# Norms of two query heads in one run, and their scale moved from the scores to the exponential

## The reference, cut to what matters

```
def rmsnorm(x, g, eps=EPS):
    var = jnp.mean(jnp.square(x), axis=-1, keepdims=True)
    return x * jax.lax.rsqrt(var + eps) * g
scale = 1.0 / np.sqrt(D)
q = (hidden_states @ Wq).reshape(B, Sq, H, D)
k = (encoder_hidden_states @ Wk).reshape(B, Skv, H, D)
v = (encoder_hidden_states @ Wv).reshape(B, Skv, H, D)
q = rmsnorm(q, gq)
k = rmsnorm(k, gk)
scores = jnp.einsum('bqhd,bkhd->bhqk', q, k) * scale
attn = jax.nn.softmax(scores, axis=-1)
out = jnp.einsum('bhqk,bkhd->bqhd', attn, v)
return out.reshape(B, Sq, H * D) @ Wo
```

## Time and profile before

| | us |
|---|---|
| median of 3 runs | 1866.22 (1866.08 to 1866.52) |
| the profiled execution | 1869.1 |
| its span | 1867.3 |
| PE busy | 1758.7 (94%) |
| DVE busy | 1317.8 (71%) |
| ACT busy | 955.9 (51%) |
| POOL busy | 663.5 (36%) |

### The profile page before, as it was taken

The page is one execution under the profiler, slowest core; times in us unless marked ns, Lnnn a source line. Parts: engine busy times, 40 slices in busy tenths (PEclk is TensorE's granted clock), DMA queues, the critical chain, the costliest instruction groups (busy, mean ns, idle before and its releaser), DMA issues.

```text
span 1867.3 us, 19387 instructions
## 1 busy us (share of the span) xinstructions
PE 1758.7 (94%) x6054; PEld 801.7 (43%) x6054; DVE 1317.8 (71%) x1919; ACT 955.9 (51%) x1904; POOL 663.5 (36%) x693
## 2 busy tenths in 40 slices
PE   8878769989999999999999999999999899999999
PEld 2323233434444344444444544444444344454543
DVE  3978877998998799889887989987643444422221
ACT  6867875656563555575456565564435233330100
POOL 1324522345472244456432464562123333310100
PEclk9989889999999899999999999999999999999999
DMA  8999933688771146697312589841112799846110
GB/s 267 260 289 291 300 109 98 173 211 215 189 195 46 48 102 155 160 266 196 102 31 70 129 199 234 212 109 62 41 47 78 215 301 256 246 141 241 68 51 28
DMA packets 163173, 300.30 MB, mean 161 GB/s; under 512 B 18936, under 2 KB 51704, under 8 KB 160128
## 3 DMA queue, kind: packets, MB, share of 16 engines
q1 hardware_dynamic: 145792, 236.14, 40.3%
q0 software_dynamic: 17280, 62.92, 17.5%
HBM read 177.64 MB, written 58.33 MB: 126 GB/s over the span
## 4 chain that ended last, share of the span: by engine, by line
PE 62%; DVE 18%; issue 6%; ACT 5%; DMA 5%; POOL 2%; SPq 2%; DVEq 0%; ACTq 0%; POOLq 0%
PE p L799 9%; PE p L776 8%; PE p L759 8%; PE p L810 8%; PE p L846 6%; DVE s_M L963 5%; PE p L652 4%; PE p L782 4%; PE p L861 3%; DVE s_M L958 2%; PE p L699 2%; DVE s_M L968 2%; PE p L733 2%; DMA s_bc<-bc_scratch 1%; PE p L738 1%
## 5 line engine op out<-in xcount | busy, mean ns | idle before, releaser
L963 DVE TENSOR_TENSOR_SCAN s_M<-s_M 128x1024 f32<-128x1024 f32 x128 | 296.8, 2319 | 7.8 <-ACT s_M L1218 5.3
L1106 DVE CUSTOM_DVE_ANT_0 s_U<-p,s_U 128x512 f32<-128x512 f32 x256 | 187.3, 745 | 162.8 <-PE p L776 161.5
L776 PE MATMUL p<-s_U 128*128 128x512 f32 x512 | 269.3, 614 | 5.6 <-DVE s_U L1106 2.8
L759 PE MATMUL p<-s_U 128*128 128x512 f32 x512 | 253.7, 604 | 4.7 <-DMA s_U<-in_Wq 2.1
L1445 POOL DMA_DIRECT2D s_u<-s_M x120 | 112.6, 938 | 391.5 <-DVE s_M L968 368.8
L1490 POOL TENSOR_SCALAR s_U<-s_U 128x512 f32<-128x512 f32 x256 | 229.4, 917 | 6.3
L810 PE MATMUL p<-s_U 128*128 128x512 f32 x512 | 224.0, 593 | 0.0
L799 PE MATMUL p<-s_U 128*128 128x512 f32 x472 | 213.6, 593 | 2.6 <-ACT s_U L1348 2.5
L1348 ACT COPY s_U<-p 128x512 f32<-128x512 f32 x196 | 105.3, 592 | 189.7 <-PE p L782 188.4
L1218 ACT ACTIVATE s_M<-s_dl,s_small 128x511 f32<-128x511 f32 x256 | 170.3, 718 | 40.3 <-DVE s_M L963 36.8
L1343 ACT ACTIVATE s_U<-s_U 128x512 f32<-128x512 f32 x256 | 181.6, 710 | 5.3
(11 more groups left out here) (171 smaller groups left out, 2364.3 us busy)
## 6 DMA issues: line engine op xcount, KB each, us to landing
s_u<-s_M POOLq DMA_DIRECT2D x120, 512.0 KB, 7.6
s_bc<-bc_scratch SPq DMA_DIRECT2D x128, 256.0 KB, 5.0
k_scratch<-s_U SPq DMA_DIRECT2D x16, 1024.0 KB, 9.4
v_scratch<-s_U SPq DMA_DIRECT2D x16, 1024.0 KB, 7.8
s_U<-in_Wq SPq DMA_DIRECT2D x64, 256.0 KB, 6.9
s_U<-k_scratch SPq DMA_DIRECT2D x64, 256.0 KB, 5.2
s_U<-rk_scratch SPq DMA_DIRECT2D x64, 256.0 KB, 5.5
s_U<-in_Wo SPq DMA_DIRECT2D x64, 256.0 KB, 4.5
```

Source lines behind the costliest of these rows:

```text
L759: ins = e.matmul(banks[bk][:], wqq[j % 2][:, k, :], axT[b % 2][:, k, :], start=(k == 0), stop=(k == 3))
L776: e.matmul(banks[bk][:], qT[j % 3][:, k * 128:(k + 1) * 128], kT[j % 2], start=True, stop=True).then_inc(S["a_s"], 1)
L963: e.tensor_tensor_scan(w, dA[i % 2], w, 0.0, ALU.mult, ALU.add).then_inc(S["m_s"], 1)
L1106: e.tensor_tensor_reduce(out=Pm[j % 2][:, k, :], in0=banks[ABANK[kind, j, k]][:], in1=rkb[j % 2], scale=rq[:, k:k + 1], scalar=-3.0e38, op ...
```

## The change

Norms are made for two neighbouring heads at a time. The "nq" step of an even head j sums the squares of j and j+1: eight matmuls, with a stationary that has ones in column 0 for the first head and in column 1 for the second (`only`), accumulate into the same four blocks of one bank, so that row 32t + i holds head j+i. One transpose, one copy of eight columns and one power of eight columns follow. The step moves from iteration j-1 to iteration j, behind the query of j+1.

The scores no longer take the query's norm: DVE multiplies with the keys' norms alone, and the maximum is that of the raw scores. The exponential gets the norm as its per-row scale. Its bias is the maximum times the negated norm, made for each tile by itself right before its exponential; for this the eight norms of a pair are negated once by ACT (`nrq`). Each exponential waits for its own maximum and no longer for all four.

Two buffers for squares are kept, and the first two heads use `PT` for them; `ones`, `krs` and `mhalf` move or shrink. The query weights are loaded at the last "q" step. In `context()` the costs of "nq", "nt" and "ex" change and in `experts()` some dependences are added.

```
-ATTN = [x for j in range(2) for x in [("q", j, k) for k in range(4)] + [("nq", j, 0), ("nt", j, 0)][:2 - 2 * j]]
+ATTN = [("q", j, k) for j in range(2) for k in range(4)]
...
-        ATTN += [(("nq", "nt")[t], j + 1, 0)] if j + 1 < NJ and t < 2 else [("q", j + 2, t - 2)] if j + 2 < NJ and t > 1 and not late else []
+        ATTN += ([(("nq", "nt")[t], j, 0)] if j < NJ and j % 2 == 0 else []) if t < 2 else [("q", j + 2, t - 2)] if j + 2 < NJ and not late else []
...
-"nq": [("PE", 0.35), ("ACT", 0.4)], "nt": [("PE", 0.2), ("ACT", 0.3), ("POOL", 1.1)], "ex": [("ACT", 0.95 if k else 1.35)]
+"nq": [("PE", 1.1), ("ACT", 0.4)], "nt": [("PE", 0.2), ("ACT", 0.3), ("POOL", 1.3)], "ex": [("ACT", 1.3)]
...
-            needs.append((NB, "s", NJ - 2, 3))
+            needs += [(NB, "s", NJ - 2, 3)] + ([("E", 1)] if p == 2 else [])
+        if kind == "gu" and ex == 0 and 0 < p < 4:
+            needs.append(("E", len(out) - 1))
...
                     elif kind == "nq":
-                        e.wait_ge(S["a_qs"], j + 1)
-                        for t in range(4):
-                            ins = e.matmul(banks[bk][32 * t:32 * t + 32, 0:128], ones[:], sq[:, t * 128:(t + 1) * 128], start=True, stop=True)
+                        e.wait_ge(S["a_qs"], j + 2)
+                        if j == 0:
+                            e.wait_ge(S["f_pad"], 4)
+                        for i in range(2):
+                            for t in range(4):
+                                ins = e.matmul(banks[bk][32 * t:32 * t + 32, 0:128], only[i], squares(j + i)[:, t * 128:(t + 1) * 128], start=(i == 0), stop=(i == 1))
...
-                            e.wait_ge(S["a_rq"], j + 1)
-                        e.tensor_tensor_reduce(..., scale=rq[:, k:k + 1], ...)
+                        e.tensor_tensor_reduce(..., scale=1.0, ...)
...
                     elif kind == "ex":
+                        c = 2 * k + j % 2
                         if k == 0:
-                            e.wait_ge(S["a_mx"], 4 * j + 4)
-                            e.activation(nm, mx, ACT.Copy, scale=-1.0).then_inc(S["a_m"], 1)
+                            if j % 2 == 0:
+                                e.wait_ge(S["a_rq"], j // 2 + 1)
+                                e.activation(nrq, pair_norms(j), ACT.Copy, scale=-1.0).then_inc(*v.up())
+                                e.wait_ge(*v.now())
                             if j >= 3:
                                 e.wait_ge(S["a_rc"], j - 2)
-                            e.wait_ge(S["a_m"], j + 1)
-                        e.activation(Pm[j % 2][:, k, :], Pm[j % 2][:, k, :], ACT.Exp, bias=nm[:, k:k + 1], scale=1.0, accum_out=sm[:, k:k + 1]).then_inc(S["a_e"], 1)
+                        e.wait_ge(S["a_mx"], 4 * j + k + 1)
+                        e.activation(nm[:, k:k + 1], mx[:, k:k + 1], ACT.Copy, scale=nrq[:, c:c + 1]).then_inc(S["a_m"], 1)
+                        e.wait_ge(S["a_m"], 4 * j + k + 1)
+                        e.activation(Pm[j % 2][:, k, :], Pm[j % 2][:, k, :], ACT.Exp, bias=nm[:, k:k + 1], scale=pair_norms(j)[:, c:c + 1], accum_out=sm[:, k:k + 1]).then_inc(S["a_e"], 1)
...
-                    if kind == "nq" and j + 2 < NJ:
+                    if kind == "q" and k == 3 and j + 2 < NJ:
                         e.wait_ge(S["a_q"], j + 1)
                         load_wq(j + 2)
```

More of the change, by code:

```diff
@@ L23 @@
 NW = 3
-UW = 27744
+UW = 28264
 SEMS = """
@@ L500, in flamingo @@
         onesf = U[:, 27136:27264]
+        ones = onesf[:, 0:32]
+        krs = U[:, 27264:27520]
         ipw = du[:, 0:2, :]
@@ L548, in flamingo @@
         qT = [U[:, 25600 + 512 * i:26112 + 512 * i] for i in range(3)]
-        sq = U[:, 27136:27648]
-        aq = U[:, 27648:27744]
+        sq = [U[:, 27136 + 512 * i:27648 + 512 * i] for i in range(2)]
+        aq = U[:, 28160:28256]
+        only = [U[:, 7104 + 32 * i:7136 + 32 * i] for i in range(2)]
         wd = {n: A[n].rearrange("(k p) n -> p k n", p=128) for n in ("Wq", "Wk", "Wv", "Wo")}
@@ L561, in head_stats, with pair_norms, squares @@
         def head_stats(j):
-            return [aq[:, 32 + 20 * (j % 3) + 4 * i:36 + 20 * (j % 3) + 4 * i] for i in range(5)]
+            return [aq[:, 32 + 16 * (j % 3) + 4 * i:36 + 16 * (j % 3) + 4 * i] for i in range(4)]
+        def pair_norms(j):
+            return aq[:, 80 + 8 * (j // 2 % 2):88 + 8 * (j // 2 % 2)]
+        nrq = U[:, 28256:28264]
+        def squares(j):
+            return PT[:, j, :] if j < 2 else sq[j % 2]
         ew = [wq[:, :].bitcast(F32)] + [U[:, 6144 * i:6144 * (i + 1)] for i in range(3)]
@@ L743, in pe_keys @@
                         for h in range(4):
-                            ins = e.matmul(banks[bk][32 * h:32 * h + 32, :], ones[:], ksq[h], start=True, stop=True)
+                            ins = e.matmul(banks[bk][32 * h:32 * h + 32, :], ones, ksq[h], start=True, stop=True)
                         ins.then_inc(S["k_n"], 1)
@@ L1105, in dve_attn @@
                         e.wait_ge(S["a_s"], 4 * j + k + 1)
-                        e.tensor_tensor_reduce(out=Pm[j % 2][:, k, :], in0=banks[ABANK[kind, j, k]][:], in1=rkb[j % 2], scale=rq[:, k:k + 1], scalar=-3.0e38,
+                        e.tensor_tensor_reduce(out=Pm[j % 2][:, k, :], in0=banks[ABANK[kind, j, k]][:], in1=rkb[j % 2], scale=1.0, scalar=-3.0e38,
                                                op0=ALU.mult, op1=ALU.max, accum_out=mx[:, k:k + 1]).then_inc(S["a_mx"], 1)
@@ L1330, in act_attn @@
+                        if j == 2:
+                            e.wait_ge(S["d_rk"], 64 * NB)
+                        e.activation(squares(j), banks[bk][:], ACT.Square).then_inc(S["a_qs"], 1)
+                    elif kind == "nq":
+                        e.wait_ge(S["a_nq"], j // 2 + 1)
+                        if j:
+                            e.wait_ge(S["a_nt"], j // 2)
                         e.activation(nqs[:], banks[ABANK[kind, j, k]][:, 0:128], ACT.Copy, bias=EPS, scale=1.0 / HD).then_inc(S["a_nqs"], 1)
@@ L1399, in setup @@
             def setup():
-                e.memset(ones[:], 1.0).then_inc(S["p_set"], 1)
                 e.memset(onesf, 1.0).then_inc(S["p_set"], 1)
@@ L1455, in pool_ffn @@
                             e.memset(xb[:, 512:640], 0.0).then_inc(S["f_pad"], 1)
+                            e.memset(U[:, 7104:7168], 0.0).then_inc(S["f_pad"], 1)
+                            e.wait_ge(S["f_pad"], 2)
+                            for i in range(2):
+                                e.memset(only[i][:, i:i + 1], 1.0).then_inc(S["f_pad"], 1)
                         deviation(qt[:, 1:2], (S["f_rv"], 8 * b + t + 1), "f_rs")
@@ L1563, in setup @@
                 load_x(0)
-                e.wait_ge(S["p_set"], 8)
+                e.wait_ge(S["p_set"], 7)
                 for ch in range(4):
```

48 lines of the change are left out of this document (21 added, 27 removed).

## The result

The kernel after takes 1897.2 us (1889.2 to 1898.2, 4 runs) where the kernel before takes 1866.4 (1866.1 to 1867.0, 4 runs). The ratio is 1.0153, 95% interval 1.0134 to 1.0172: some 28.6 us slower. The forecast was 1873.8, its range 1849 to 1891.

A forecast was written before the change was run, and what follows sets the result against it. PE was taken to bound the kernel. Norm runs -13.4, old waits -7.5, PE's waits for ACT +25.5 and late POOL norms +3 sum to +7.6 us on 1866.2, giving 1873.8 us, range 1849 to 1891.

The forecast's parts named there:

- the credit for TensorE: On PE: -13.4 us for fewer norm runs and transposes over 32 pairs, and -7.5 us for their waits.
- the old waits: PE's waits before norm runs (7.2 us) and transposes (2.9) mostly vanish: -7.5 us, bounds 0 and -10.
- POOL's +3: Heads where POOL's power comes late for a pair's first exponential: +3 us, bounds 0 and +19.
- A norm run of 0.81 us: On PE: a pair's norm run of twice as many passes takes 0.81 us, bounds 0.55 and 1.10.
- in series: Rival: a pair's norm run on PE takes the 1.10 us of two runs, +9.3 us, 1883; chance 0.09.
- PE's busy time falls by 10 to 14: Sign that the forecast is right: PE's total busy time falls by 10 to 14 us.
- ACT's part of 4.80 in the first head of a pair: On ACT: four scalings and exponentials take 4.80 us a head instead of 3.15, +1.65.
- ACT stays covered: Rival: scaling plus exponential stay below about 1.03 us, so the norm run doesn't wait; 1851, chance 0.27.
- Where ACT's time lands: In pairs of heads without FFN work, PE waits 1.7 us a pair for ACT; 15 pairs, +25.5 us.
- POOL's power of 8 columns, 1.63: On POOL: the power of a pair's 8 columns takes 1.63 us, between 4 and 16 columns.
- The draw: Rival: waits are half the forecast's, 12 us, or the order moves other work into them; 1866 to 1868, chance 0.15.
- my count of 15 pairs fails first: Caveat: if the recomputed engine order regroups the heads without FFN work, the 15 pairs behind +25.5 us fail first.

The follow-up runs named there:

- e7: Kernel before with only the norms paired, old exponential part and its old planned costs, norm factors left out: 1869.7 us, ratio 1.0014.
- e1: Kernel after, its order kept, with the exponential part of the kernel before, norm factors left out: 1879.2 us, ratio 1.0082.
- e3: Kernel before, work unchanged, with the planned cost of an exponential set to 1.3 us: 1876.6 us, ratio 1.0062.
- e11: Same as e7, with the FFN placed ahead of attention on ACT by one letter of the plan: 1860.0 us, ratio 0.9970.
- e12: Kernel before with one letter of the plan moved, placing the FFN ahead of attention on ACT: 1878.5 us, ratio 1.0059.
- e4: Kernel after, work unchanged, with the old planned costs of the exponential and 0.6 for the norm run: 1885.2 us, ratio 1.0118.
- e5: Kernel before with raw scores and the norm scale at the exponential, planned 1.3 us, norms still per head: 1900.5 us, ratio 1.0181.
- e10: Kernel after, unchanged, run again: 1900.7 us, ratio 1.0186.
- e8: Kernel after with one letter of the plan moved, placing the FFN ahead of attention on ACT: 1880.9 us, ratio 1.0070.
- e13: Kernel before, work unchanged, with 0.05 us added to the planned exponentials: 1871.8 us, ratio 1.0032.
- e6: Kernel after with a head's four biases made by one DVE operation at the first exponential's place, planned costs adapted: 1901.5 us, ratio 1.0188.
- e9: Same as e6, with the DVE bias operation right behind the head's fourth scores operation and planned costs edited: 1900.7 us, ratio 1.0187.

## Why the prediction was wrong

The step that failed is the credit for TensorE: "-13.4" for the norm runs and "-7.5" for the old waits went into the sum of the end time at full size, whatever order the plan would write. In the order of before's costs the pairing brought nothing, +0.14% (0.9999 to 1.0030, e7), and nothing at 1.3 us (+0.20%, e1 against e3). With the FFN first it brought 0.89%, 17 us, about what I had (e11 against e12).

In a straight line through the table, by the first column, the parts are: pairing +0.14% = +2.6 us (e7), the exponential part 1.04% = +19.4 (e4), the order of the planned costs 0.35% = +6.5, together 28.5. My sum had -20.9, +28.5 with POOL, and nothing for the order. Of the 21 us between the forecast's +7.6 and the measured 28.6, the credit was 23.5 too good, the order missing by 6.5, and the ACT terms, POOL's +3 with them, 9 too dear. By the second column the same 28.5 are: the letter on the work of before +11, pairing -17, exponential part +18, planned costs +0.6 and the letter taken back +15.5. So only the exponential part has one price, 13 to 22 us; what the pairing is worth can't be parted from the order.

Point by point:

- *A norm run of 0.81 us.* PE in order of time in the kernel after:

```profile
1452.17 0.64 PE L782 MATMUL p<-s_U 128*32 128x128 f32 x16 [0.45 <-ACT s_U L1342]
1452.75 1.12 PE L792 MATMUL p<-s_U 128*128 128x512 f32 x2
1453.71 0.27 PE L786 MATMUL p<-s_identf,s_nqs 128*128 128x128 f32 x1
```

  The next run starts 0.58 us after it, where it was 0.36, so eight more passes cost 0.22 and the run 0.55 + 0.22 = 0.77. Confirmed, and "in series" falls. In the middle of this run 12 of its matmuls and 4 of its weight loads are in flight in the same 0.02 us:

```profile
1452.44:1452.46 0.02, 0.02 (x12) 0.02 (x4) 1.00 1.22 307
```

  The Trainium skill, "TensorE: Matmul & The Clock Gate", "Part 3: Packing small matmuls", has a weight load overlap matmuls only where the row group differs. The trace doesn't agree: the row group is the same for all 16 passes here, and they don't stand in series.
- *PE's busy time falls by 10 to 14.* It fell by 16.6 in the kernel after and 10.1 in e7, and by 7.5 to 9.0 between executions of equal clock. The work did go away, if a little less of it.
- *What ate it.* One candidate is the chain through the scans: a batch's queries need the FFN, which needs the scans. From the start of the last scan to the first exponential of head 48 it takes 194 us in the kernel before (1241 to 1435) and 195 to 205 in e3, e5 and e12, which keep the norms per head. It takes 181 to 184 in e11, e7, e1, the kernel after and e10, which pair them and whose scans are 10 to 40 us late: PE has less left to put between. But the time doesn't follow the scans one for one. In e8 the last scan starts 23 us sooner than in the kernel after (1254 for 1276) and head 48 only 11 (1450 for 1460), in 196 us. And in e7, 8.6 of the 9 us of new idle time lie ahead of the last scan and match the transposes' waits for POOL's products. That speaks for POOL in e7, and for the scans in the dry turn of the kernel after. But e11 has nearly the same waits for POOL, and there the credit came. No run moved the scans or POOL alone, so the cause of the lost credit stays open.
- *The old waits.* In e7 the norm runs wait 1.3 us in place of 7.2, and their transposes 0.0 in place of 2.9: 8.8 gone, more than the -7.5. But 9 us came up at POOL's products in the same kernel. I had asked of POOL only whether the norms are late, not its products.
- *ACT's part of 4.80 in the first head of a pair.* 4.79. Exponentials of 0.80 and scalings of 0.30: 0.81 and 0.29. The Trainium skill, "ScalarE: Activation LUTs", "What ACT_TABLE_LOAD costs", gives 799 ns, as an estimate, for an exponential with two columns by its 93 ns each; the trace agrees, 813. So both columns cost, and "ACT stays covered" falls at its own condition, a step of 1.03 (here 1.14).
- *Where ACT's time lands: 1.7 us a dense pair, 27.3 in place of 26.0.* The pair of the earlier trace rows takes 27.56 us in place of 26.00, as foreseen. But the next pair, with an output projection of 14 us in it, takes 40.33 in place of 40.25. Both pairs, from one first exponential to the next, in the kernel before

```profile
806.24:832.24 26.00, 25.97 (x99) 12.57 (x99) 24.15 (x29) 19.22 (x45) 16.95 (x17) 1.00 0.95 250
832.24:872.49 40.25, 39.85 (x131) 18.66 (x131) 36.72 (x43) 21.96 (x48) 19.89 (x21) 1.00 0.80 207
```

  and after:

```profile
805.57:833.13 27.56, 26.02 (x99) 12.63 (x98) 23.80 (x29) 21.37 (x50) 16.73 (x15) 1.00 0.94 253
833.13:873.46 40.33, 39.51 (x131) 18.79 (x130) 35.63 (x40) 24.13 (x54) 18.52 (x18) 1.00 0.79 196
```

  PE's idle time rises by 1.5 us in the first and by 0.4 in the second. I had priced the first kind and multiplied by 15, and every second dense pair is of the other kind. Over the whole kernel PE waits for the square 11.5 us and for the output's copy 6.2 (0 before), 17.7 where my sum had 25.5 for the dense heads alone. At the end the exponential part costs 13 to 22 us.
- *POOL's power of 8 columns, 1.63.* 1.64 at least, 1.65 in the median of all 48 powers, those of 16 columns included. ACT does wait for it, 16.3 us in 11 of the 32 pairs (0.3 in e7), but 12.3 of them in the last batch, where PE is idle for only 1.3 us more than before. What they cost at the end is not shown.
- *The draw.* "Waits half of mine" gives -13.4 - 7.5 + 12.75 + 3 = -5.2, 1861, and not the 1866 to 1868 that I wrote beside it. Its chance of 0.15 stood for a time that its own condition doesn't give.
- *"The order of all engines is computed anew" and "my count of 15 pairs fails first".* I named it and gave it no term and only a share in the draw's chance. It did not regroup the dense heads: the pairs above follow each other as before. It moved the FFN and the scans. At unchanged work an order alone costs 6.5 to 13 us (e3, and e4 against the kernel after and e10).

What stays open: why a given order puts the passes late. One letter of the plan acts with opposite signs in two kernels (e8, e12), and 5% on one cost moved one kernel by 6 us (e13), so the share of the order that belongs to the 1.3 us as such, and not to any edit, isn't settled. With the FFN first the 1.3 costs nothing. Nor is it settled how much of the pairing's lost credit is POOL's products and how much the passes, or what the DVE bias would give in a good order (e6, e9).

## What to carry to other kernels

Where a plan writes the order of every engine, an edit of a planned cost is a change of its own: measure it on the old work first, and give it a term and a chance. Time taken off the busiest engine counts at the end only where no other wait takes its place. Before crediting it, ask which engine is late next (here POOL with its products) and when the work of the next stretch is ready (here the last scan of a pass). A price read from one iteration holds for iterations of its kind: count the kinds before multiplying. Give a helper engine's new operation a place in its queue by what is ahead of it there, not by its own 0.2 us.

## What the runs showed of the hardware

- A scale column beside a bias column adds 103 ns to a 128x512 exponential (710 to 813 ns, 256 each); a copy of one column, 128x1, with a scale column takes 285 ns.
- The scores operation on DVE falls from 745 ns to 685 when its scale is the constant 1 in place of a column: 60 ns, 15.4 us over 256. No run shows what it is worth at the end; DVE waits 137.3 us for PE ahead of these operations in the kernel after.
- The kernel before spread from 1860.1 to 1872.5 us over the four groups of runs, where its first four had agreed within 1 us. A single run can lie 0.4% off the median. In the last group the run of 1860.1 was granted a clock of 0.984 and the one of 1872.5 0.979.
